# Experts' weights in eight rotating buffers, without filler copies, and read as rows of 2 KB

## The reference

```
logits = xf @ w_cls.T
scores = softmax(logits)
_, topk_idx = top_k(scores + bias, 8)
w = take(scores, topk_idx);  w = w / (w.sum() + EPS) * 1.5
buf[e, pos] = x of the tokens of expert e      # pos < 256
g, u = split(buf @ w_gate_up[e])               # 512 -> 2 x 256
y = (silu(g) * u) @ w_down[e]                  # 256 -> 512
out[token] += w_r * y * (1 + w_z.sum())
```

## Time and profile before

| | us |
|---|---|
| median of 3 runs | 1022.58 |
| the runs | 1023.45, 1015.96, 1022.58 |
| profiled execution, its own time | 1025.01 |
| profiled execution, span of the trace | 1023.2 |

### The profile page before, as it was taken

One profiled execution on the slowest core, in us unless ns is written; L12 is line 12 of the kernel. 1 busy time (PEld: TensorE's weight loads), 2 busy tenths in 40 slices (PEclk: granted clock), 3 DMA queues, 4 the chain that ended last, 5 costly groups with the idle time before them and its releaser, 6 DMA issues. The chain is left out here.

```text
span 1023.2 us, 14443 instructions
## 1 busy us (share of the span) xinstructions
PE 905.2 (88%) x4313; PEld 731.7 (72%) x4313; DVE 771.3 (75%) x1837; ACT 503.7 (49%) x867; POOL 495.9 (48%) x420
## 2 busy tenths in 40 slices
PE   5789999999999999999699999999379897687960
PEld 3577888888888888888488888888357575566740
DVE  6978888888888888888777777776768767485720
ACT  5455555555555554555642333332258766475730
POOL 2456676666667666666400000000065566656652
PEclk9989999999999999999999999999679989797985
DMA  8001111111111111103755654431189979798743
GB/s 295 6 32 47 57 41 53 47 57 42 58 47 57 37 58 47 56 33 104 264 171 184 254 184 146 145 105 54 44 287 280 321 218 283 212 276 235 184 61 41
DMA packets 52758, 131.01 MB, mean 128 GB/s; under 512 B 12156, under 2 KB 14588, under 8 KB 46528
## 3 DMA queue, kind: packets, MB, share of 16 engines
q1 hardware_dynamic: 41248, 114.67, 32.4%
q0 software_dynamic: 11424, 15.29, 8.6%
HBM read 106.53 MB, written 35.91 MB: 139 GB/s over the span
## 5 line engine op out<-in xcount | busy, mean ns | idle before, releaser
L595 POOL TENSOR_TENSOR a_t<-a_t 128x512 f32<-128x512 f32 x80 | 105.2, 1315 | 101.7 <-DVE a_t L358 101.7
L1081 DVE TENSOR_TENSOR w_l<-raw,w_h 128x1024 fp32r<-128x1024 f32 x96 | 114.7, 1222 | 13.5 <-ACT w_h L1074 13.2
L604 POOL TENSOR_TENSOR a_fQ<-a_fQ,a_den 128x512 f32<-128x512 f32 x64 | 88.0, 1376 | 71.8 <-DVE a_den L396 71.8
L213 PE MATMUL a_PQ<-w_h,a_xT_h 128*128 128x512 f32 x384 | 107.8, 403 | 10.0 <-DVE w_l L345 9.3
L775 PE MATMUL r_PY<-w_h,r_o_h 128*128 128x512 f32 x256 | 106.3, 415 | 3.4 <-DVE r_o_l L867 3.4
L1179 POOL DMA_INDIRECT out<-m_y,si x38 | 66.2, 1741 | 88.0 <-DMA out<-m_y,si 64.5
L1051 POOL TENSOR_SCALAR r_vr<-r_mv 128x1 f32<-128x1 f32 x16 | 8.4, 526 | 199.0 <-DVE r_mv L878 199.0
L213 PE MATMUL a_PQ<-w_l,a_xT_h 128*128 128x512 f32 x384 | 104.2, 394 | 0.0
L213 PE MATMUL a_PQ<-w_h,a_xT_l 128*128 128x512 f32 x384 | 103.5, 392 | 0.0
L775 PE MATMUL r_PY<-w_l,r_o_h 128*128 128x512 f32 x256 | 101.9, 398 | 0.0
L775 PE MATMUL r_PY<-w_h,r_o_l 128*128 128x512 f32 x256 | 101.8, 398 | 0.0
(11 more groups left out here) (168 smaller groups left out, 2193.8 us busy)
## 6 DMA issues: line engine op xcount, KB each, us to landing
raw<-in_wgu SPq DMA_DIRECT2D x32, 1024.0 KB, 6.8
oT<-a_o SPq DMA_DIRECT2D x64, 256.0 KB, 2.5
raw<-in_wd SPq DMA_DIRECT2D x32, 512.0 KB, 6.4
v_l<-oT SPq DMA_DIRECT2D x11, 1024.0 KB, 6.6
v_h<-oT SPq DMA_DIRECT2D x5, 1024.0 KB, 6.7
out<-r_x SPq DMA_DIRECT2D x18, 256.0 KB, 2.0
a_xin<-in_x SPq DMA_DIRECT2D x16, 256.0 KB, 3.2
v_l<-in_wq SPq DMA_DIRECT2D x4, 1024.0 KB, 12.4
```

What stands on the lines that cost most here:

```text
L213: last = eng.matmul(bank[:, :], a[:, k, :], w[:, 4 * i + k, :], start=s == 0 and k == 0, stop=s == 2 and k == 3)
L595: eng.tensor_tensor(t1[:, r % 2, :], t1[:, r % 2, :], t2[:, r % 2, :], ALU.add).then_inc(sm["xr"], 1)
L604: eng.tensor_tensor(q, q, den[:, n % 2, :].unsqueeze(2).broadcast_to([P, 4, P]), ALU.mult).then_inc(sm["fs"], 1)
L1081: eng.tensor_tensor(low, src, high.bitcast(F32), ALU.subtract).then_inc(sm["m_wl"], 1)
```

## The change

- Eight rotating sets of weights (`ring`, RING = 8) in place of three. A set is a raw up part (4 blocks), a raw down part (2 blocks) and the low parts, which DVE writes over the raw ones in place. Sets 0 to 2 take the room of raw, sets 3 to 6 that of w_l (free once Wo's last product is done), and set 7 blocks 20 to 23 of w_h and a small tensor of its own. The high parts rotate as before.
- A set is free when the matmuls of expert e-8 are done (m_gu for up, m_yd for down), no longer when its split is.
- In routing, SP loads experts 0 to 2 as before, the up part of 7 in chunk 5, those of 3 and 4 as soon as Wo's last product is done (r_y), ahead of the last store_w, and those of 5 and 6 behind it.
- Weights are read in the layout in which they are given: 128 partitions times 4 (up) or 2 (down) rows of 2 KB, where it was one row of 8 or 4 KB.
- no_scatter and its filler copy go. All scatters bump one semaphore m_s; for an expert with one half the scatter bumps it by 32. The wait for the scatter before now stands behind the gathers, right ahead of the scatter. The end of the stage is awaited by SP instead of POOL.
- The second gather of e+6 no longer waits for the one of e in the same buffer.
- PE does up(0) ahead of turn(1); all other iterations keep their order.
- DVE does all six clears first; ACT waits for m_ident only after its split of the up part of expert 1.

```diff
+RING = 8
+def load_up(sm, eng, ring, wgu, e):
+    up, _, _, _ = ring[e % RING]
+    eng.dma_start(up, wgu[e].rearrange("k p f -> p k f")).then_inc(sm[f"m_wg{e % RING}"], 16)
+def load_down(sm, eng, ring, wd, e):
+    _, down, _, _ = ring[e % RING]
+    eng.dma_start(down, wd[e].rearrange("k p f -> p k f")).then_inc(sm[f"m_wd{e % RING}"], 16)
+def parts(ring, w_h, e, part):
+    up, down, up_l, down_l = ring[e % RING]
...
 routing, SP:
                     if 2 <= c < 5:
-                        e = c - 2
-                        eng.dma_start(raw[e][:, 0:4, :], wgu[e]).then_inc(sm[f"m_wg{e}"], 16)
-                        eng.dma_start(raw[e][:, 4:6, :], wd[e]).then_inc(sm[f"m_wd{e}"], 16)
+                        load_up(sm, eng, ring, wgu, c - 2)
+                        load_down(sm, eng, ring, wd, c - 2)
+                    if c == 5:
+                        load_up(sm, eng, ring, wgu, 7)
                 for t in range(2):
                     eng.dma_start(out[T + t * P:T + (t + 1) * P, :], x2[:, 1, :]).then_inc(sm["r_so1"], 16)
+                eng.wait_ge(sm["r_y"], NC)
+                for e in (3, 4):
+                    load_up(sm, eng, ring, wgu, e)
+                    load_down(sm, eng, ring, wd, e)
                 store_w(NC - 1)
+                for e in (5, 6):
+                    load_up(sm, eng, ring, wgu, e)
+                    load_down(sm, eng, ring, wd, e)
...
 experts, SP:
                 eng.wait_ge(sm["m_g01"], 16)
-                for e in range(3, NE):
-                    eng.wait_ge(sm["m_wl"], 3 * (e - 3) + 2)
-                    eng.dma_start(raw[e % 3][:, 0:4, :], wgu[e]).then_inc(sm[f"m_wg{e % 3}"], 16)
-                    eng.wait_ge(sm["m_wl"], 3 * (e - 3) + 3)
-                    eng.dma_start(raw[e % 3][:, 4:6, :], wd[e]).then_inc(sm[f"m_wd{e % 3}"], 16)
+                load_down(sm, eng, ring, wd, 7)
+                for e in range(RING, NE):
+                    for t in range(2):
+                        eng.wait_ge(sm[f"m_gu{t}"], e - RING + 1)
+                    load_up(sm, eng, ring, wgu, e)
+                    for t in range(2):
+                        eng.wait_ge(sm[f"m_yd{t}"], e - RING + 1)
+                    load_down(sm, eng, ring, wd, e)
+                eng.wait_ge(sm["m_s"], 32 * NE)
...
 experts, POOL:
-                def no_scatter(e):
...
-                def scatter(e, t):
+                def scatter(e, t, done):
                     i = 2 * e + t
-                    if t == 0 and e >= 1:
-                        eng.wait_ge(sm["m_s0"], 16 * e)
-                        eng.wait_ge(sm[f"m_s1{(e - 1) % 2}"], 16 * ((e + 1) // 2))
                     eng.wait_ge(sm[f"m_y{t}"], e + 1)
...
                 for e in range(NE):
-                    no_scatter(e)
                     if e + 6 < NE:
                         gather(e + 6, 0)
                         gather(e + 6, 1)
-                    scatter(e, 0)
+                    load_flag(eng, regs, e)
+                    if e >= 1:
+                        eng.wait_ge(sm["m_s"], 32 * e)
                     with eng.If_lt(regs[e % 7], T):
-                        scatter(e, 1)
+                        scatter(e, 0, 16)
+                        scatter(e, 1, 16)
+                    with eng.Else():
+                        scatter(e, 0, 32)
...
 experts, PE:
                     both(eng, regs, e - 1, turn_a, "m_at1")
+                    if e == 0:
+                        both(eng, regs, 0, up, "m_gu1")
                     both(eng, regs, e + 1, turn, "m_xt1")
-                    both(eng, regs, e, up, "m_gu1")
+                    if e > 0:
+                        both(eng, regs, e, up, "m_gu1")
                     both(eng, regs, e - 1, down, "m_yd1")
...
 host:
-        "wgu": np.asarray(L0_ffn_w_gate_up).reshape(NE, 4, P, 512).transpose(0, 2, 1, 3),
-        "wd": np.asarray(L0_ffn_w_down).reshape(NE, 2, P, 512).transpose(0, 2, 1, 3),
+        "wgu": np.asarray(L0_ffn_w_gate_up).reshape(NE, 4, P, 512),
+        "wd": np.asarray(L0_ffn_w_down).reshape(NE, 2, P, 512),
```

More of the change, by code:

```diff
@@ L628, in _, with routing @@
                         rstd(c + 1)
-def routing(nc, sm, x, wo, wc, bias, consts, oT, xn2d, out, gi, si, raw, wgu, wd, w_h_, w_l_, v_h, v_l):
+def routing(nc, sm, x, wo, wc, bias, consts, oT, xn2d, out, gi, si, ring, wgu, wd, w_h_, w_l_, v_h, v_l):
     with ExitStack() as ctx:
@@ L967, in _ @@
                     else:
[L968 removed]
+                        split_low(sm, eng, ring, w_h_, 0, 0)
                     xT_low(c)
@@ L1056, in _, with pair, split_high, split_low @@
                     rstd(c)
-def part_of(raw, w, e, part):
-    if part < 2:
[L1063 to L1069, removed]
+RING = 8
[5 more added lines that the diff above has]
+    eng.dma_start(down, wd[e].rearrange("k p f -> p k f")).then_inc(sm[f"m_wd{e % RING}"], 16)
+def pair(ap):
+    return ap.rearrange("p k t -> p (k t)")
+def parts(ring, w_h, e, part):
+    up, down, up_l, down_l = ring[e % RING]
+    if part < 2:
+        i = 4 * (e % 3) + 2 * part
+        k = slice(2 * part, 2 * part + 2)
+        return pair(up[:, k, :]), pair(w_h[:, i:i + 2, :]), pair(up_l[:, k, :])
+    i = 12 + 2 * (e % 4)
+    return pair(down), pair(w_h[:, i:i + 2, :]), pair(down_l)
+def split_high(sm, eng, ring, w_h, e, part):
     if part != 1:
         kind = "m_wd" if part == 2 else "m_wg"
-        eng.wait_ge(sm[f"{kind}{e % 3}"], 16 * (e // 3 + 1))
-    src, high = part_of(raw, w_h, e, part)
+        eng.wait_ge(sm[f"{kind}{e % RING}"], 16 * (e // RING + 1))
+    src, high, _ = parts(ring, w_h, e, part)
     eng.activation(high, src, ACT.Copy).then_inc(sm["m_wh"], 1)
-def split_low(sm, eng, raw, w_h, w_l, e, part):
+def split_low(sm, eng, ring, w_h, e, part):
     eng.wait_ge(sm["m_wh"], 3 * e + part + 1)
-    src, high = part_of(raw, w_h, e, part)
-    src, low = part_of(raw, w_l, e, part)
+    src, high, low = parts(ring, w_h, e, part)
     eng.tensor_tensor(low, src, high.bitcast(F32), ALU.subtract).then_inc(sm["m_wl"], 1)
-def experts(nc, sm, wgu, wd, xn2d, out, gi, si, raw, consts, w_h, w_l):
+def experts(nc, sm, wgu, wd, xn2d, out, gi, si, ring, consts, w_h, w_l, v_h):
     with ExitStack() as ctx:
@@ L1101, in experts @@
         y = sb("y", [P, 4, 2, D])
-        spare = sb("spare", [1, 2, 16])
+        with nc.sbuf_tensor("m_raw", [P, 2, 512], F32) as raw:
+            pass
+        low = sb("low", [P, 2, 512], F32R)
         ident = sb("ident", [P, P])
@@ L1108, in experts @@
         PY = [ps("PY0"), ps("PY1")]
+        ring = ring + [(v_h[:, 20:24, :], raw[:, :, :], w_h[:, 20:24, :], low[:, :, :])]
         def f(ap):
@@ L1283, in clear @@
                     eng.memset(xg[:, i, 1, :], 0.0).then_inc(sm["m_xg"], 1)
-                clear(0)
-                clear(1)
+                for i in range(6):
+                    clear(i)
                 w_low(1, (0, 1))
@@ L1289, in _ @@
                 both(eng, regs, 0, x_low, "m_xTl1")
-                for i in range(2, 6):
-                    clear(i)
                 w_low(1, (2,))
@@ L1318, in w_high @@
                     for part in parts:
-                        split_high(sm, eng, raw, w_h, e, part)
+                        split_high(sm, eng, ring, w_h, e, part)
                 def x_high(e, t):
@@ L1372, in build @@
         si = ctx.enter_context(nc.sbuf_tensor("si", [P, 64], U32))
-        raw = [ctx.enter_context(nc.sbuf_tensor(f"raw{i}", [P, 6, 512], F32)) for i in range(3)]
-        routing(nc, sm, x, wo, wc, bias, cr, oT, xn2d, out, gi, si, raw, wgu, wd, w_h, w_l, v_h, v_l)
-        experts(nc, sm, wgu, wd, xn2d, out, gi, si, raw, cr, w_h, w_l)
+        with nc.sbuf_tensor("raw", [P, 18, 512], F32) as raw:
+            pass
+        low = ctx.enter_context(nc.sbuf_tensor("low", [P, 18, 512], F32R))
+        ring = [(v[:, i:i + 4, :], v[:, i + 4:i + 6, :], w[:, i:i + 4, :], w[:, i + 4:i + 6, :])
+                for v, w, n in ((raw, low, 3), (v_l, w_l, 4)) for i in range(0, 6 * n, 6)]
+        ring7 = ring + [(v_h[:, 20:24, :], None, None, None)]
+        routing(nc, sm, x, wo, wc, bias, cr, oT, xn2d, out, gi, si, ring7, wgu, wd, w_h, w_l, v_h, v_l)
+        experts(nc, sm, wgu, wd, xn2d, out, gi, si, ring, cr, w_h, w_l, v_h)
 def kernel(L0_attn_x, L0_attn_Wq, L0_attn_Wk, L0_attn_Wv, L0_attn_Wo, L0_ffn_w_cls, L0_ffn_bias,
```

38 lines of the change are left out of this document (15 added, 23 removed).

## The result

The changed kernel takes 1028.85 us (median of 4 runs, 1028.25 to 1030.4), the kernel before 1019.27 beside it (4 runs, 1015.6 to 1023.45): a ratio of 1.012 with a 95% interval of 1.008 to 1.016. Forecast were 977 us and a range of 967 to 1003. It is slower by about 10 us.

What follows compares the result with a forecast made beforehand. The prediction took the chain of scatters, slowed by weight loads in POOL's DMA queue, to bound the kernel. From 1025.0 us, stalls -38.0, tail -12.7 and start +3 gave 977.3, so 977, with a range of 967 to 1003.

Steps and rivals of the forecast that it cites:

- What bounds the kernel: Expert stage: late scatters make gathers late and stop PE; 58.7 us hang on the chain of scatters.
- Rows of 2 KB: Scatter chain beside loads: 2 KB packets cost 0.088 us a turn, not 0.235; scatters 6.2 us apart.
- an excess of 3.8: Scatter intervals beside loads: 3.8 us lost per expert, against up to 5.2 if queues take turns packet by packet.
- Rival (a): Scatter chain: small rows buy nothing in turns; intervals 7.15 instead of 7.9 us, kernel 1001 us; chance 0.25.
- No filler copies: POOL's in-order stream: 26 issues at 1.15 + 0.3 us leave, little gained alone; 0 to -2.
- PE does up(0) before turn(1): Start of the expert stage: second act of expert 0 at 761.8; +3 us, from -1 to +5.
- Stalls: Experts 4 to 31: time beyond what compute alone needs, 38.0 us, all forecast to go (-38.0).
- tail: From PE's end to the last scatter: 20.7 us of backlog, 8 us of it kept, so -12.7.
- Eight buffers: Weight loads: experts 3 to 6 move to routing; worth nothing directly, DMA work fits with about 5 us to spare.
- rival (b): Weight loads: weights come late; at 280 GB/s the kernel takes 1006 us; chance 0.13, of which 0.05 slower than before.
- The store of w, m_ident and the clears: End of routing: the store's delay is covered, m_ident's load behind weight loads costs 0 to +2, the clears 0.
- The chances: Whole kernel: forecast 0.62; faster by over 1% 0.90, within 0.05, slower 0.05.

Runs made afterwards that it cites:

- Experiment 7: Experiment 5 without the loads of experts 8 to 31, whose splits read old buffers, so the output is not the reference's; 970.78 us, ratio 0.955.
- experiment 1: The changed kernel with weights in rows of 8 and 4 KB instead of 2 KB; 1028.2 us, ratio 1.009.
- experiment 2: The kernel before with weights read in rows of 2 KB, all else as before; 1016.24 us, ratio 0.9974.
- 12: Experiment 9 with weights in rows of 8 and 4 KB instead of 2 KB; 985.62 us, ratio 0.969.
- experiment 9: As experiment 6, but the semaphore that releases the load is bumped by a one-element memset behind the scatter; 987.03 us, ratio 0.968.
- experiment 3: The changed kernel with POOL's branch on the second half ahead of the wait for the scatter before; 1012.81 us, ratio 0.995.
- Experiment 5: The changed kernel with POOL's branch ahead of the wait and PE's old order at expert 0; 1006.08 us, ratio 0.990.
- experiment 6: As experiment 5, the load of expert e+8 released by POOL's semaphore increment right behind the scatter of e; 1043.7 us, ratio 1.027.
- experiment 8: The kernel before without filler copies, with one semaphore for scatters and the branch behind the wait; 1028.01 us, ratio 1.010.
- experiment 4: The changed kernel with PE's old order, turn(1) ahead of up(0); 1022.92 us, ratio 1.004.

## Why the prediction was wrong

**What bounds the kernel** was read rightly: the chain of scatters, slowed by weights, with PE and ACT waiting for it. Experiment 7 reaches 970.8 with the weights gone, so what the sums of 38.0 and 12.7 us describe was there to be had (it has neither the branch behind the wait nor the new order of PE). The forecast of 977 was, in effect, the time of a kernel whose weights hardly slow the scatters.

**The step that failed** is *Rows of 2 KB*: "The same turn costs 0.088 instead of 0.235". It took the shape of a bound that fitted (5.2 us against an excess of 3.8) for a mechanism. Intervals stayed at 8.86 and 7.75 us in place of 6.2, and rows of either width give the same time to within 3 us in three pairs of kernels (1 and after, 2 and before, 12 and 9). What the runs show in its place: the excess hangs on the moment of the load against that of the scatter, 8.87, 6.51 and 7.49 us for a load posted with it, 1.7 us and 5 us behind it. A load that is in front goes first, and the scatter's first packet, which comes at 2.2 us without loads, comes at 5.4, 2.6 and 4.3 us. Rival (a) came nearest: 7.15 us between scatters, since one DMA of four leaves the queue; experiments 3 and 5, the change without its branch, have 7.19 and 7.10. That it is met so closely is partly luck, as the kernel before and experiment 2 read 7.89 and 7.55 for a difference of 2.8 us. Its 1001 us is 12 under the 1012.8 of experiment 3, 3 of which are the start. The rule of the Trainium skill under it (DMA: Bandwidth & Descriptors, on queues, rings and completion order: an engine drains a group of descriptors ahead of another queue) points the right way: the packet records show a load in front going ahead of the scatter in bulk, with either width of rows. Its typical size fits less well. By 17 descriptors of 2 KB a turn would end after 1.5 us (an estimate from the page's figure and the prediction's 0.088 us). In experiment 6 the scatter waits 3.2 us beyond the 2.2 at which it could start, while 0.97 MB pass, some 30 rows for each of the 16 engines; that is more than 17 and within the page's limit of 64. The records do not name the engine, so single turns can't be seen.

**A term that was missing**, and the one that made the sign: the branch behind the wait. The change says in its own words that the wait stands "right ahead of the scatter", and the diff has `If_lt` between the two. The step *No filler copies* counted issues that leave POOL ("Bounds 0 to -2") and asked under which landing POOL's work hides. But work between a landing and the next issue hides under nothing. It measured +16 us (experiment 3), 0.56 us a link. Against the copies' own gain of 4 to 7 it leaves the loss of 9 to 12 in experiment 8, and so the sign of the result. The prediction asked of every edit what hides it, and never what stands between a landing and the next issue.

**PE does up(0) before turn(1)**: the mechanism was right, and the second act of expert 0 stood at 762.41, forecast 761.8. The size was +3. The silu of expert 4 shows +5.6, of which 3.7 go with the old order (experiment 4; 789.75 against 786.09 in 3 and 5 is the same 3.7); experiment 1, also with the new order, shows only +2.3. The kernel's time gives back 6. The other 1.9 are not of the order; PE's first turn is 0.9 us later. The step named the rest as the end of its range: +5 "if PE, idle for almost 5 us, is granted 1.2 GHz again". It idled for 4.5 us and the clock fell, in all three profiles with that order; the sum had taken the other case.

**Stalls** (-38.0) and **tail** (-12.7): +3.9 and -2.3, both following from the interval. The end gave 3.1 that had no term; 1.3 of it is the step from experiment 8's end, awaited by POOL, to that of the changed kernel, awaited by SP.

**Eight buffers** give nothing directly, as forecast: splits idle for 0.1 and 0.3 us, so rival (b), weights that come late, didn't occur, and the slower bandwidth of 2 KB rows had no price that a pair of runs shows. The "about 5 us to spare" did not follow from the step's own numbers, 183 us at 1.04 being just the 190 that were needed. With the rest of the change they are part of the 5 us between experiments 4 and 8. What they are good for is that they allow experiment 9: loads can be held back until a moment that suits the scatters.

**The store of w, m_ident and the clears** have no run that prices them by themselves; the first turn of PE stands at 746.32 in the changed kernel and at 745.41 in the one before, so 0 to +2 for m_ident is not contradicted.

**The chances** went wrong in one place: 0.05 on slower, all of it put on late weights. A link of the serial chain that gets longer was no rival, though the change rewrites just that link 31 times.

## What to carry to other kernels

Where DMAs follow each other in a chain (each waits for the landing of the last), everything between the landing and the next issue counts in full, once a link. Take branches, register reads and flags ahead of the wait, even if the code must be written twice, and read in the chain of waits what stands there. In these runs a load in bulk from another queue cost such a chain by when it was posted, not by its rows or by its share of the bandwidth: let a small instruction behind the critical DMA release it, so that it fills the gap. And a cost model that fits one number isn't a mechanism; move one part of it (here, rows of the kernel before) ahead of relying on it.

## What the runs showed of the hardware

- A semaphore increment by POOL behind an indirect DMA does not wait for that DMA's issue: in experiment 6 the load that it releases is issued at 850.54, and the scatter's row runs from 850.74 to 852.36. A memset behind it starts about 1.05 us after the DMA's start (790.56 and 791.60) and was the better signal: 1043.7 against 987.0 us.
- A scatter of POOL's queue posted in the same moment as 1.5 MB of another queue takes 8.87 us until the next can go; alone it takes 4.9 to 5.1. Its first packet starts 5.4 us behind its issue in place of 2.2, and 1.24 MB of the load have started by then.
- One register branch between a wait and a DMA of POOL costs 0.56 to 0.62 us (7.75 against 7.19 and 5.51 against 4.89 between scatters).
- Experiments 9 and 12 take 3.2 and 3.1% less than the kernel before. Experiment 5 has 1.0 of these; the rest comes with the moment at which loads are posted. Experiments 6 and 9, which differ by that moment alone, are 57 us apart.
- PE's clock, at 2.4 GHz in 755 to 760 after the slow start, fell to 1.2 GHz again in a gap of 4.5 us without work (0.63 and 0.69 granted in the two windows that follow).
